# Reordering VectorE's and ScalarE's work in a fused gated-scan and expert kernel, with the last residual moved from GpSimd to VectorE

## What is computed

```python
g = sigmoid(einsum('bld,ed->ble', x, Wg) + bg)
h = scan over l of  h = (1 - g) * h + g * x
attention = einsum('bld,ed->ble', h, Wo) + bo
# experts: xf is (16384, 256), E = 8 experts, C = 320 places each, H = 1024
eid = argmax(softmax(xf @ router_w + router_b))
rank = position of the token among those of its expert;  valid = rank < C
y_tok = relu(xf @ w1[eid] + b1[eid]) @ w2[eid] + b2[eid]      # valid tokens
yov   = relu(xf @ ow1 + ob1) @ ow2 + ob2                      # all others
ffn = where(valid, y_tok, yov)
x = x + layernorm(attention(layernorm(x)))
x = x + layernorm(ffn(layernorm(x)))
```

## Time and profile before

| | |
|---|---|
| median of 3 runs | 1272.75 us (1271.8 to 1273.87) |
| profiled execution, its own time | 1271.02 us |
| its span from first to last instruction | 1269.3 us |
| mean granted clock of TensorE | 0.98 |
| TensorE matmuls, busy | 1172.6 us, 92% of the span, 7705 instructions |
| VectorE, busy | 1003.3 us, 79% |
| GpSimd, busy | 810.3 us, 64% |
| ScalarE, busy | 772.5 us, 61% |
| residual2 on GpSimd (L437) | 32 instructions, 76.9 us, 2.40 each |

### The profile page before, as it was taken

The page is one execution under the profiler, slowest core; times in us unless marked ns, Lnnn a source line. Parts: engine busy times, 40 slices in busy tenths (PEclk is TensorE's granted clock), DMA queues, the critical chain, the costliest instruction groups (busy, mean ns, idle before and its releaser), DMA issues. The chain is left out here.

```text
span 1269.3 us, 24820 instructions
## 1 busy us (share of the span) xinstructions
PE 1172.6 (92%) x7705; PEld 1038.1 (82%) x7705; DVE 1003.3 (79%) x2731; ACT 772.5 (61%) x1362; POOL 810.3 (64%) x887
## 2 busy tenths in 40 slices
PE   4499999999999999999999999999999999889994
PEld 4388888888888888888888888888888888789994
DVE  4688888888888888888888888888888876578882
ACT  4265666666666666666666666666665655477773
POOL 4456666666666666666666666666666664436774
PEclk9699999999999999999999999999999999999997
DMA  7211111111111110100111110011111100334430
GB/s 242 83 35 50 51 47 44 38 37 34 33 33 33 33 33 33 33 26 24 33 33 33 33 33 25 25 33 33 33 33 33 33 17 18 104 112 168 149 103 31
DMA packets 59688, 65.32 MB, mean 51 GB/s; under 512 B 7836, under 2 KB 55886, under 8 KB 59525
## 3 DMA queue, kind: packets, MB, share of 16 engines
q1 hardware_dynamic: 52484, 59.58, 14.5%
q0 software_dynamic: 7168, 5.32, 1.4%
HBM read 40.17 MB, written 38.87 MB: 62 GB/s over the span
## 5 line engine op out<-in xcount | busy, mean ns | idle before, releaser
L362 POOL TENSOR_TENSOR rstd<-veps,mhalf 128x4 f32<-128x4 f32 (+1 forms) x144 | 179.4, 1246 | 355.1 <-DVE nmean L712 355.1
L539 ACT ACTIVATE hid<-psH,biasT 128x512 f32<-128x512 f32 (+1 forms) x320 | 209.1, 653 | 264.4 <-PE psH L1010 259.2
L1108 PE MATMUL psY<-W_hi,hid_hi 128*128 128x256 f32 x1216 | 351.2, 289 | 0.9 <-DVE hid_lo L833 0.9
L1111 PE MATMUL psY<-W_hi,hid_lo 128*128 128x256 f32 x1216 | 344.2, 283 | 0.0
L1110 PE MATMUL psY<-W_lo,hid_hi 128*128 128x256 f32 x1216 | 344.0, 283 | 0.0
L833 DVE TENSOR_TENSOR hid_lo<-hid,hid_hi 128x512 fp32r<-128x512 f32 (+1 forms) x320 | 266.0, 835 | 89.3 <-ACT hid_hi L543 83.8
L1008 PE MATMUL psH<-xfT_hi,W_hi 128*128 128x512 f32 (+1 forms) x640 | 246.1, 385 | 5.5 <-DVE xfT_lo L777 2.9
L1010 PE MATMUL psH<-xfT_hi,W_lo 128*128 128x512 f32 (+1 forms) x640 | 242.5, 379 | 0.0
L1009 PE MATMUL psH<-xfT_lo,W_hi 128*128 128x512 f32 (+1 forms) x640 | 242.3, 379 | 0.0
L1108 PEld LDWEIGHTS psY<-W_hi,hid_hi 128*128 128x128 f32 x1216 | 230.2, 189 | 10.5 <-DVE hid_lo L833 1.8
L1110 PEld LDWEIGHTS psY<-W_lo,hid_hi 128*128 128x128 f32 x1216 | 230.0, 189 | 6.7
(11 more groups left out here) (110 smaller groups left out, 2186.6 us busy)
## 6 DMA issues: line engine op xcount, KB each, us to landing
xin<-L_attn_x SPq DMA_DIRECT2D x32, 512.0 KB, 3.5
stage<-L_ffn_w SPq DMA_DIRECT2D x16, 1024.0 KB, 6.2
out<-outt SPq DMA_DIRECT2D x32, 512.0 KB, 2.9
xbuf<-zrow SPq DMA_DIRECT2D x1, 2570.0 KB, 18.5
xin<-xbuf SPq DMA_DIRECT2D x8, 257.0 KB, 5.5
stage<-L_ffn_ow SPq DMA_DIRECT2D x2, 1024.0 KB, 10.3
xbuf<-x,idx POOLq DMA_INDIRECT x128
b_b<-L_ffn_b SPq DMA_DIRECT2D x1, 1024.0 KB, 13.5
```

Of the source, the lines that this page charges most:

```text
L362: pool.tensor_tensor(rstd[k][:, 0:n], veps[k][:, 0:n], mhalf[:, 0:n], ALU.pow).then_inc(s_rs[k], 1)
L539: act.activation(hid[j % 2][:, 0:n], psH[:, j % 2, 0:n], ACT.Relu, bias=bias).then_inc(s_hid, 1)
L1108: pe.matmul(psY_t[:, t, :], hi, w[0][:, j, :], start=(j == 0 and t % 2 == 0), stop=False, skip_group_check=True)
L1111: last = pe.matmul(psY_t[:, t, :], lo_, w[0][:, j, :], start=False, stop=(j == HC - 1), skip_group_check=True)
```

## The change

On VectorE `stats1` moves from behind chunk 2 to directly behind `attended`, `residual2` of the previous group is added behind it, `place` moves from behind chunk 3 and `xn_lo` to behind chunk 2, `residual1` and the reading half of `stats2` come behind chunk 3, then `xn_lo`, then the rest of `stats2`, and only then chunks 4 and 5. On GpSimd `residual2` is gone. On ScalarE `norm1` comes ahead of `xn_hi`, both behind chunk 3. On TensorE the rank matmuls come at j = 3. The last group's residual is added by VectorE behind chunk 4 of the first expert.

```diff
 # gpsimd, step
                 if live(far, NG):
                     norm0(far)
-                if live(prev, NG):
-                    residual2(prev)
                 if live(nxt, NG):
                     deviation(1, nxt, TG)
...
             norm2((0, 1), xe, ET, NG)
-            residual2(last_group)
             keep_rows((0, 1))
 # scalar, step
                 hidden(range(2, 4))
+                if up:
+                    norm1(nxt)
                 if ahead:
                     xn_hi(far)
                 hidden(range(4, 5))
-                if up:
-                    norm1(nxt)
 # vector
+            def residual2(g):
+                i, v = g
+                dve.wait_ge(s_z, cnt(g, 1, 1))
+                if live(grp(i, v, -2), NG):
+                    dve.wait_ge(s_st_out[v], landed(grp(i, v, -2)))
+                dve.tensor_tensor(outt[v][:], ysb[:], x1[v][:, :, 0:D], ALU.add).then_inc(s_out, 1)
+
+            def read_rows2a(g):
+                dve.wait_ge(s_x1, cnt(g, 1, 1))
+                read_rows(2, lambda t: x1[g[1]][:, t, 0:D], TG)
+
             def stats2(g):
-                dve.wait_ge(s_x1, cnt(g, 1, 1))
-                stats(2, lambda t: x1[g[1]][:, t, 0:D], g, TG)
+                read_rows2a(g)
+                moments(2, g, TG)
 # vector, step
                 if up:
                     attended(nxt)
+                    stats1(nxt)
+                if live(grp(i, u, -1), NG):
+                    residual2(grp(i, u, -1))
                 low(2)
+                if run:
+                    place(now)
+                low(3)
                 if up:
-                    stats1(nxt)
-                low(3)
+                    residual1(nxt)
+                    read_rows2a(nxt)
                 if ahead:
                     xn_lo(far)
-                if run:
-                    place(now)
-                low(4)
                 if up:
-                    residual1(nxt)
-                    stats2(nxt)
-                low(5)
+                    moments(2, nxt, TG)
+                low(4, 5)
 # vector, estep
+                    if j == 4 and not live(prev, E):
+                        residual2((NG // 2 - 1, 1))
 # tensor, step
-                        if j == 4:
+                        if j == 3:
                             rank(now)
```

More of the change, by code:

```diff
@@ L430, in step @@
                     state_lo(far)
[L432 to L437, removed]
             norm0((0, 0))
```

## The result

The changed kernel takes **1252.49 us** (median of 4, 1250.81 to 1254.17), the kernel before 1272.28 in the same comparison: ratio 0.9843, 95% interval 0.9826 to 0.986. It is faster by 19.8 us (1.6%), where 42.3 were forecast; the predicted 1230.5 and the range up to 1251 were missed, by 1.5 at the range's end. The profiled execution took 1254.17 (span 1252.4).

The account below looks back on a forecast made before the run. TensorE was taken as the bound, losing 1.21 us a step at transposes waiting for GpSimd. Savings of 31.8 steady, 4.1, 1.5, 0.9 and 4.0 sum to 42.3, giving 1230.5 us; range 1222 to 1251.

Parts of the forecast that it names:

- the middle of the bounds: GpSimd's power behind VectorE's new residual: forecast to run 625.58 to 627.51, between ends at 626.6 and 628.1.
- waits for hid_lo 2 as well: Late bound for GpSimd's power after attention's statistics: it ends at 628.1, with 0.75 lost at the gate.
- rival B: Power ends at 628.1, its product is caught behind hid_lo 3; gate loses 1.7 a step, 1277 us; chance 0.08.
- times up to the gate can be kept: TensorE work before the gate is unchanged, so the old step's times up to the gate at 634.06 hold.
- steps 30, 31 and the experts: End of the run: savings of 4.1 at step 30, 1.5 at step 31, 0.9 and 4.0 in the first two experts.
- A: Power waits for the residual and hid_lo 2; gate loses 0.75 a step, 24.3 saved, 1248 us; chance 0.20.
- C: Something later in the step, hid_lo 6 or 7, stops TensorE for the whole amount: 1261 to 1273 us; chance 0.06.
- 0.66: Chance given to the forecast itself, 1230.5 us, with its own range of 1225 to 1240.

Follow-up runs that it names:

- Dispatch first: The changed kernel with this step's dispatch moved ahead of the second norm on GpSimd; 1228.95 us, ratio 0.9666 against the kernel before.

## Why the prediction was wrong

**What it had right.** The direction; that the wait at the transposes vanishes in full; hid_lo 2 at 0.68 (0.69 forecast); VectorE's residual at 1.23; the power behind it, for which the middle of the bounds was taken: 1.93, as forecast. The bound "waits for hid_lo 2 as well" didn't occur, nor did rival B's late product. The shared port as the Trainium skill has it ("SBUF — State Buffer", section "Who interferes with whom") and the trace agree on this power, 1.93 behind the add; the sum had used for it.

**The step that failed** is the sentence "Dispatch (four indirect DMAs on GpSimd's queue) and state_lo follow as now, all 2.2 earlier against the next step's project", with the one it rests on, "times up to the gate can be kept". It failed twice. First in size: the second norm was kept at 3.79 though it was moved to lie wholly beside VectorE's recurrence (632.83 to 637.03), and there it takes 5.65. So the dispatch came 0.4 earlier and not 2.2. With 2.2 its last DMA would have ended some 0.8 ahead of the end of layer 2 (an estimate, from the 1.37 behind it before); whether that is early enough no run of the changed order on this chip tells. Second in kind: the move was booked as harmless, without asking what the DMAs would then run beside. They were the one moved item whose neighbours were not listed. Ending 0.8 instead of 1.4 behind layer 2, they go with a signal of TensorE that is 1.6 to 1.8 late and a result as late. Of that, slack on VectorE takes a part, and 0.57 or 1.3 reaches the chain to the gate, which had been costed to within 0.15. Hence 0.77 a step at the gate (0.95 from start to start), not 0.15. "Dispatch first" takes away the place alone and gives 31.85, the forecast's period.

By the sum, in the profiled executions: 16.9 of the 42.3 came. The 29 periods gave 8.6 (29 x 0.297, from 32.98 to 32.69), where 1.06 a step would have given 30.7: 22.1 is missing. The first step gave nothing (its transposes at 83.2 in both), where 1.1 was booked. The rest is the end.

**The end of the run.** From the last of these transposes to the span's end 229.6 went to 221.3, so 8.3 against 10.5 for steps 30, 31 and the experts. The second expert's 2.61 is gone (ScalarE's wait for the weight 3.5 to 0.8), and step 31's transposes wait 2.78 in place of 4.46, about as forecast. Step 30's still wait 1.54 of their 2.88, and the ones behind step 31's now wait for GpSimd where they didn't:

```profile
1060.81 1.09 PE L1069 MATMUL psT<-ident,tok 128*128 128x128 f32 x8 [1.54 <-POOL tok L403]
```

```profile
1109.95 0.88 PE L1069 MATMUL psT<-ident,tok 128*128 128x128 f32 x6 [0.93 <-POOL tok L403]
```

These terms were not taken apart by runs.

**The rivals.** The measured time is near A's 1248, and A's 0.75 a step at the gate near the 0.77 measured, but its mechanism is refuted: the power did not wait for hid_lo 2. C, "the wait only changes its name", is what happened in kind, at a place that C didn't name and for 1.05 (32.69 less 31.64) of the 1.34 us that a step of the kernel before lies above the floor of 31.64. The range was too narrow since no case had a moved DMA disturbing what it had not touched before. One slip in the chances: 0.66 and 0.20 leave 0.02 of C in the 0.88 for faster, which is not "most of C".

**What stays open.** How the dispatch delays TensorE's signals. The traces show that the signals themselves are late: the one to VectorE's result, and less so the one to ScalarE's next relu (it starts 0.29 to 0.50 behind its matmul, 0.04 in most steps before). On chip 5 moving the dispatch ends this. Rows on their way do not explain it, and whether it happens on every chip is not shown.

## What to carry to other kernels

List for every moved instruction, DMAs first, what it will run beside at its new time, and not only what waits for it. When an engine starts late with no releaser named, compare the time of the signal with the end of the work it tells of, and look for a DMA of GpSimd's queue beside it. Before a cause is read out of an experiment, see whether the hold came and went inside the unchanged trace (here the bytes a step fell to nothing and the hold stayed), and run the kernel that shows it on the same chip. And once a reordering has made slack behind a queue's entry, try the entry that feeds only later work (here the dispatch) at each end of that slack: here that brought more than the change itself.

## What was not expected of the hardware

With GpSimd's indirect DMAs across the end of layer 2, TensorE's signal comes up to 1.78 us behind the matmul it tells of, and 0.86 behind the end of GpSimd's own span in the step shown, in the first comparison and on chip 5; the other two chips show nothing of the kind. The Trainium skill, "Perfetto Trace Analysis", section "DMA Instruction — SWDGE (GPSIMD)", says that such a span ends with the descriptors, not with the data. The trace agrees: in the step shown the last span ends 0.77 behind layer 2 and the last packet 1.56, just ahead of the late signal at 1.63. But with no rows sent the packets end at 1.51 and the signal comes at 0.01. While GpSimd issues, even with no rows sent, a small VectorE instruction takes 0.36 instead of 0.16.

GpSimd's four second normalisations take 5.65 in place of 3.79 once they lie wholly beside the recurrence, a term that the forecast kept at 3.79. It is hidden behind the slack that the change makes, and no transposes wait for it in the steady part.
